# Two loads and two stores in turn with at most three transfers in flight, and two additions moved, in a group-norm and sign-weight convolution kernel

## What is computed

```python
bw = cw + stop_gradient(jnp.sign(W) - cw)          # the value is sign(W)
x = x + conv_general_dilated(_gn(x), bw, window_strides=(1, 1), padding=((1, 1), (1, 1)))
# _gn: mean and variance over a group of 2 channels x 56 x 56 pixels, eps 1e-5
```

## Time and profile before

| | us |
|---|---|
| timed runs, median of 3 | 204.43 (203.82 to 205.47) |
| the profiled execution, its own time | 206.21 |
| its span, first to last instruction | 204.4 |

### The profile page before, as it was taken

How to read it: one execution, slowest core, us unless ns; L and a number is a source line. 1 busy time by engine, 2 the same in 40 slices (tenths; PEclk the granted TensorE clock), 3 DMA queues, 4 the chain that set the end, 5 groups by cost and what they waited for, 6 DMA issues and landing times.

```text
span 204.4 us, 10027 instructions
## 1 busy us (share of the span) xinstructions
PE 191.5 (94%) x4482; PEld 168.2 (82%) x4482; DVE 165.5 (81%) x363; ACT 149.7 (73%) x142; POOL 166.7 (82%) x85
## 2 busy tenths in 40 slices
PE   1999999998999999999979999899989999999990
PEld 0587977887887887977868898799988999999990
DVE  2999999996999877999957799987769799727392
ACT  3186998899987299899429989943997999596000
POOL 1039887999999999989996988999798799999500
PEclk9999999999999999999999999999999999999997
DMA  6986878929798998988959988898887970905374
GB/s 215 373 336 207 262 244 255 305 92 323 295 314 258 352 327 282 266 246 342 305 231 251 308 246 225 340 289 259 273 247 231 232 274 3 387 18 233 120 270 174
DMA packets 18698, 52.17 MB, mean 255 GB/s; under 512 B 2080, under 2 KB 5024, under 8 KB 18656
## 3 DMA queue, kind: packets, MB, share of 16 engines
q1 hardware_dynamic: 18656, 51.54, 76.7%
HBM read 25.84 MB, written 25.69 MB: 252 GB/s over the span
## 4 chain that ended last, share of the span: by engine, by line
PE 69%; DVE 12%; ACT 10%; DMA 3%; issue 2%; POOL 1%; SPq 1%; DVEq 0%; ACTq 0%; POOLq 0%
PE psum L720 69%; DVE stats L487 4%; ACT halves L411 3%; ACT xnorm L405 3%; DMA w_raw<-in_L_conv_W_dram 3%; DVE xbuf L557 2%; DVE xbuf L543 1%; DVE xbuf L567 1%; POOL halves L320 1%; SPq L236 1%; ACT moved L424 1%; ACT line_halves L434 1%; DVE xbuf L531 1%; ACT lines_norm L438 1%; DVE own L495 1%
## 5 line engine op out<-in xcount | busy, mean ns | idle before, releaser
L720 PE MATMUL psum<-halves,w_taps 64*64 64x385 f16 (+8 forms) x4140 | 184.9, 325 | 3.2 <-issue 2.5
L720 PEld LDWEIGHTS psum<-halves,w_taps 64*64 64x64 f16 x4140 | 158.5, 107 | 21.2 <-issue 4.1
L320 POOL TENSOR_TENSOR halves<-xnorm,halves 128x784 f16<-128x784 f32 (+5 forms) x35 | 91.7, 2641 | 21.8 <-ACT xnorm L405 21.6
L487 DVE BATCH_NORM_STATS2 stats<-xbuf 128x6 f32<-128x448 f32 x112 | 60.7, 611 | 3.6 <-DMA xbuf<-in_x_dram 3.3
L411 ACT ACTIVATE halves<-xbuf,coef 128x784 f16<-128x784 f32 (+5 forms) x35 | 50.7, 1449 | 3.6 <-DVE coef L512 3.3
L405 ACT ACTIVATE xnorm<-xbuf,coef 128x784 f32<-128x784 f32 (+5 forms) x35 | 50.5, 1442 | 0.0
L424 ACT ACTIVATE moved<-psum 64x784 f32<-64x784 f32 (+1 forms) x30 | 25.5, 849 | 11.4 <-PE psum L720 10.8
L335 POOL TENSOR_TENSOR xbuf<-xbuf,moved 128x784 f32<-128x784 f32 (+1 forms) x15 | 29.4, 1957 | 2.0 <-ACT moved L424 2.0
L557 DVE SCALAR_TENSOR_TENSOR xbuf<-psum,xbuf 64x784 f32<-64x784 f32 (+1 forms) x32 | 28.2, 881 | 1.0
L543 DVE SCALAR_TENSOR_TENSOR xbuf<-psum,xbuf 128x784 f32<-128x784 f32 x21 | 20.3, 967 | 10.7 <-PE psum L720 10.7
L361 POOL TENSOR_TENSOR line_halves<-lines_norm,line_halves 128x1512 f16<-128x1512 f32 (+1 forms) x10 | 20.9, 2121 | 0.5 <-ACT lines_norm L438 0.2
(11 more groups left out here) (36 smaller groups left out, 72.5 us busy)
## 6 DMA issues: line engine op xcount, KB each, us to landing
xbuf<-in_x_dram SPq DMA_DIRECT2D x48, 448.0 KB, 4.9
out_dram<-xbuf SPq DMA_DIRECT2D x43, 392.0 KB, 4.7
xbuf<-in_x_dram SPq DMA_DIRECT2D x16, 224.0 KB, 5.1
out_dram<-xbuf SPq DMA_DIRECT2D x5, 504.0 KB, 5.9
out_dram<-xbuf SPq DMA_DIRECT2D x5, 448.0 KB, 3.2
out_dram<-xbuf SPq DMA_DIRECT2D x5, 364.0 KB, 5.3
out_dram<-xbuf SPq DMA_DIRECT2D x5, 252.0 KB, 5.0
out_dram<-xbuf SPq DMA_DIRECT2D x1, 224.0 KB, 2.9
```

The source lines that it names most:

```text
L320: nc.gpsimd.tensor_tensor(at(halves[:, k % HRING, 1, :], a, b), at(xnorm[:, k % NRING, :], a, b), at(halves[:, k % HRING, 0, :], a, b), AL ...
L487: nc.vector.bn_stats(stats[:, n, :], xbuf[:, s, n * STAT:(n + 1) * STAT]).then_inc(blocks_ready, 1)
L720: mm = pe.matmul(outs[:, :, left:right], weights, ins[:, :, left + dx:right + dx], start=first_step, stop=last_step)
```

## The change

- SP: the pieces of a pair are loaded two at a time. In loop k: pieces 0 and 1 of pair k+3 (when TensorE has finished the away blocks before pair k), then the two stores of the second half of pair k-1 (`store_unit(k - 1, 1)`), then pieces 2 and 3 (when two away blocks of pair k are done), then the two stores of the first half of pair k.
- SP: before each of these transfers it waits until the third last one has landed (`ended[-3]`), so that at most three are in flight. For that every store has a semaphore of its own (`stored[s][n]`), and the waits on them are by part. The last three stores of the last pair are not paced.
- SP: the loads of pair 2 are paced too; before, two of its pieces were issued with those of pair 1 and two later.
- `WINOGRAD` pairs are stored in other pieces: rows 43 to 56, 0 to 16, 16 to 34 and 34 to 43.
- GpSimd: where pair k is in `WINOGRAD` and pair k-2 is not (k = 3, 6, 9, 12), `add_away(k - 2, 1)` comes behind the chunks `lo(k, c)` instead of ahead of them.
- VectorE: in loop 1, three of the seven statistics of pair 3 come behind `add_home(1, 0)` and `add_away(1, 0)` instead of ahead.

The diff, its core:

```diff
@@ -181,7 +181,7 @@
         psum = ctx.enter_context(nc.psum_tensor("psum", [128, 8, 512], F32))
 
         loaded = [[sem(f"loaded{s}_{p}") for p in range(NPIECE)] for s in range(XRING)]
-        stored = [sem(f"stored{s}") for s in range(XRING)]
+        stored = [[sem(f"stored{s}_{n}") for n in range(5)] for s in range(XRING)]
         w_loaded = sem("w_loaded")
         w_signed = sem("w_signed")
         ident_step = sem("ident_step")
@@ -242,11 +242,18 @@
             sp.dma_start(w_raw[:], w.rearrange("o c h w -> o (c h w)")).then_inc(w_loaded, 16)
             for n in range(NPIECE):
                 start_load(sp, 1, n)
-            for n in range(2):
-                start_load(sp, 2, n)
-            def store(k, a, b):
-                sp.dma_start(at(both(out, k), a, b), at(xbuf[:, k % XRING, :], a, b)).then_inc(stored[k % XRING], 16)
+            ended = [(loaded[1][n], 16) for n in range(NPIECE)]
+            def load(k, n):
+                sp.wait_ge(*ended[-3])
+                start_load(sp, k, n)
+                ended.append((loaded[k % XRING][n], landed(k)))
+            def store(k, n, a, b):
+                sp.dma_start(at(both(out, k), a, b), at(xbuf[:, k % XRING, :], a, b)).then_inc(stored[k % XRING][n], 16)
 
             def wait_away(k, i):
                 u = away_before(k) + i
@@ -255,56 +262,59 @@
                 else:
                     sp.wait_ge(away_done, 2 * aways_before(u + 1))
 
-            def store_part(k, n):
+            def paced_store(k, n, a, b):
+                sp.wait_ge(*ended[-3])
+                store(k, n, a, b)
+                ended.append((stored[k % XRING][n], landed(k)))
+            def store_unit(k, i):
                 if k in WINOGRAD:
-                    if n == 0:
+                    if i == 0:
                         sp.wait_ge(home_done, home_before(k) + 1)
-                        store(k, WROW + WROWS, H)
-                    elif n == 1:
-                        wait_away(k, 0)
-                        store(k, 0, 16)
-                    elif n == 2:
-                        sp.wait_ge(home_done, home_before(k) + 3)
-                        store(k, WROW, WROW + WROWS)
-                    else:
-                        wait_away(k, 1)
-                        store(k, 16, WROW)
+                        paced_store(k, 0, WROW + WROWS, H)
+                        return
+                    wait_away(k, 0)
+                    paced_store(k, 1, 0, 16)
+                    sp.wait_ge(home_done, home_before(k) + 3)
+                    wait_away(k, 1)
+                    paced_store(k, 2, 16, WROW + 9)
+                    paced_store(k, 3, WROW + 9, WROW + WROWS)
                     return
-                sp.wait_ge(home_done, home_before(k) + n // 2 + 1)
-                wait_away(k, n // 2)
-                store(k, 14 * n, 14 * n + 14)
-            def wait_part(k, n):
-                if k in WINOGRAD and n == 3:
-                    sp.wait_ge(home_conv, home_blocks_before(k, 1) + 2)
-                elif k + n > 0:
-                    sp.wait_ge(away_conv, away_blocks_before(k) + n)
+                sp.wait_ge(home_done, home_before(k) + i + 1)
+                wait_away(k, i)
+                paced_store(k, 2 * i, 28 * i, 28 * i + 14)
+                paced_store(k, 2 * i + 1, 28 * i + 14, 28 * i + 28)
+            for n in range(NPIECE):
+                load(2, n)
             for k in range(NP):
-                for n in range(NPIECE):
-                    new = k + AHEAD
-                    if new < NP:
-                        if new >= XRING:
-                            sp.wait_ge(stored[new % XRING], 64 * (new // XRING))
-                        wait_part(k, n)
-                        start_load(sp, new, n)
-                    if n < 3 and k >= 1:
-                        store_part(k - 1, n + 1)
-                    elif n == 3:
-                        store_part(k, 0)
-                    elif n >= 1:
-                        start_load(sp, 2, n + 1)
-            store_part(LAST, 1)
+                new = k + AHEAD
+                if new < NP:
+                    if new >= XRING:
+                        for n in range(4):
+                            sp.wait_ge(stored[new % XRING][n], landed(new - XRING))
+                    if k:
+                        sp.wait_ge(away_conv, away_blocks_before(k))
+                    load(new, 0)
+                    load(new, 1)
+                if k >= 1:
+                    store_unit(k - 1, 1)
+                if new < NP:
+                    sp.wait_ge(away_conv, away_blocks_before(k) + 2)
+                    load(new, 2)
+                    load(new, 3)
+                store_unit(k, 0)
             for n, (first, rows) in enumerate(((28, 14), (42, 8), (50, 6))):
 
                 sp.wait_ge(home_done, home_before(LAST) + 2 + n)
                 sp.wait_ge(away_done, 2 * (aways_before(away_before(LAST) + 1) + 1 + n))
-                store(LAST, first, first + rows)
+                store(LAST, 2 + n, first, first + rows)
             for k in range(NP - XRING, NP):
-                sp.wait_ge(stored[k % XRING], 64 * (k // XRING + 1) + (16 if k == NP - 1 else 0))
+                for n in range(4):
+                    sp.wait_ge(stored[k % XRING][n], landed(k))
+            sp.wait_ge(stored[LAST % XRING][4], 16)
 
         @block.gpsimd
         def _(pool):
@@ -372,11 +382,14 @@
 
             for k in range(NP):
 
-                if k >= 2 and k - 2 not in WINOGRAD:
+                if k >= 2 and k - 2 not in WINOGRAD and k not in WINOGRAD:
                     add_away(k - 2, 1)
                 for c in range(len(chunks(k))):
                     if (k, c) != (0, 0):
                         lo(k, c)
+                if k >= 2 and k - 2 not in WINOGRAD and k in WINOGRAD:
+                    add_away(k - 2, 1)
                 if k == 0:
                     weights_of_products()
                 if k + 1 in WINOGRAD:
@@ -611,11 +624,16 @@
                 if k - 1 in WINOGRAD:
                     add_outer(k - 1)
                     add_away(k - 1, 1)
-                if 1 <= k < NP - 2:
+                if k == 1:
+                    pair_stats(3, range(4))
+                elif 1 <= k < NP - 2:
                     pair_stats(k + 2, range(NSTAT))
                 add_home(k, 0)
                 if k not in WINOGRAD:
                     add_away(k, 0)
+                if k == 1:
+                    pair_stats(3, range(4, NSTAT))
                 if k == 0:
                     pair_stats(2, range(NSTAT))
                 if k < NP - 2:
```

## The result

| | before | after |
|---|---|---|
| timed runs, median (range), us | 204.44 (203.82 to 208.49) | 212.68 (210.09 to 213.86) |
| the profiled execution, its own time, us | 206.21 | 213.05 |
| its span, us | 204.4 | 211.3 |

The changed kernel is slower: the ratio of the times is 1.035 [1.027, 1.043]. The direction was forecast, though narrowly; the size (206.7, with 203.4 to 210.0 as the range) was not.

What follows compares the result with a forecast made beforehand. TensorE was taken as the bound, busy 191.5 of 204.4 us. 206.21 - 3.5 + 2.5 + 2.1 = 207.3 us for an execution like the profiled one, 206.7 forecast for the runs; own range 205.0 to 208.6, overall 203.4 to 210.0.

Steps and rivals of the forecast that it cites:

- Part 1: SP's loads and stores: at most three in flight removes TensorE's three "issue" cuts, -3.5 us (bounds 0 and -3.67).
- Rival 2: Instruction fetches stay late: pacing cures nothing and the new waits come, 210.2 us; chance 0.13.
- Part 2, pair 3: Addition behind pair 3's lower halves delays loads and statistics of pair 5; TensorE pays +2.5 us at pair 4 (1.5 to 3.5).
- rival 1: The two loads behind the addition land before VectorE asks, so cuts and both waits go: 201.1 us; chance 0.13.
- landed at 3.8 or so: Pair 3: piece 3 of pair 5, issued at 52.4 us behind the first store, lands 3.8 us later, at 56.2.
- Part 2, pairs 6, 9 and 12: Moved addition delays loads, statistics and bank-freeing additions there: 0.7 us each, +2.1 us in all (bounds 0 and 1.4 each).
- Pair 9's own path: Addition ends at 117.7 us, statistics at 124.9, 1.75 late; add_inner(9) ends 1.3 later, costing pair 10 0.7 us.
- Rival 3: Only pair 3 pays; at pairs 6, 9 and 12 loads land 0.7 us sooner: 204.6 us; chance 0.14.
- Part 3: VectorE at pair 1: moving three statistics cures pair 2's 0.4 us wait, swallowed by pair 3's: 0 us, at best -0.4.
- the same 0.6 us taken off: Final sum: 207.3 us became 206.7, leaning two to one to 207.3 over 205.5 for the timed runs.

Runs made afterwards that it cites:

- e2: The kernel before with only the addition moved behind the lower halves at pairs 3, 6, 9 and 12: 210.06 us, ratio 1.028.
- e3: The changed kernel without the waits on the third last transfer; order of transfers and moved addition kept: 210.35 us, ratio 1.032.
- e5: The kernel before with only the cap of three transfers in flight added: 206.72 us, ratio 1.011.
- e12: The changed kernel with four transfers in flight for three; order and moved addition kept: 211.77 us, ratio 1.040.
- e8: The changed kernel with the addition ahead of the lower halves again at pair 3 alone: 206.9 us, ratio 1.016.
- e4: The changed kernel with SP's loads of pieces 2 and 3 put ahead of store_unit(k - 1, 1), cap kept: 202.12 us, ratio 0.989.
- e10: e4 with all seven statistics of pair 3 ahead of the additions of pair 1 again: 201.49 us, ratio 0.989.
- e11: The same kernel as e4, run again: 202.35 us, ratio 0.994.
- e6: e4 without its cap on transfers in flight: 203.66 us, ratio 1.000.

## Why the prediction was right in its path and wrong in its size

I compare by pairs, from TensorE's first matmul of a pair to that of the next, read in its timeline. A `WINOGRAD` pair takes 10.53 us where nothing stops it.

**Part 1: the size came out (-3.5 forecast, -3.8 measured) between the two profiled executions; its cause is not shown.** The ordinary pairs that had lost time to cuts (7, 10 and 11) are back at 11.82 to 11.84 us; together that is -3.8. But they are back in e2 and e3 as well, where no cap stands. And the profiled execution before was a late one, 1.78 us over its median: e1, which keeps the cap and undoes the moved addition, is at 0.997 [0.991, 1.002] of before in the timed runs, so at most 0.9% or 1.8 us was won there on balance. By the turn-taking that the Trainium skill ("DMA: Bandwidth & Descriptors", section on queues, rings and completion order) describes, this part would have been worth 0. The runs don't decide it: a packet of instructions ends ahead of each cut, but the number of transfers in flight doesn't tell which packet brings one. Rival 2 did not come true, since the cuts are gone in the changed kernel; that its 210.2 us lies nearer to 212.68 than the forecast is chance. The cap also has a price of its own, which the forecast put at nothing: e5, and pair 3 below.

**Part 2, pair 3: the path was right, the term (+2.5) mis-sized; it measured +5.5.** GpSimd's and SP's timelines of the changed kernel:

```profile
43.32 4.61 POOL L330 TENSOR_TENSOR halves<-xnorm,halves 128x1456 f16<-128x1456 f32 x2
47.89 1.85 POOL L345 TENSOR_TENSOR xbuf<-xbuf,moved 128x784 f32<-128x784 f32 x1
```

```profile
49.80 0.82 SPq L256 DMA_DIRECT2D out_dram<-xbuf  x2
50.72 1.81 SPq L236 DMA_DIRECT2D xbuf<-in_x_dram  x2
```

The addition ends at 49.74 (49.6 forecast) and refutes rival 1. The stores go out at once, piece 2 of pair 5 at 50.7 (50.45), piece 3 at 52.19 (52.4). Up to here the steps hold to within 0.3 us. VectorE's timeline, pair 3 and then pair 9:

```profile
55.09 1.15 DVE L500 BATCH_NORM_STATS2 stats<-xbuf 128x6 f32<-128x448 f32 x2 [2.92 <-DMA xbuf<-in_x_dram]
57.84 0.63 DVE L500 BATCH_NORM_STATS2 stats<-xbuf 128x6 f32<-128x448 f32 x1 [1.60 <-DMA xbuf<-in_x_dram]
58.38 0.96 DVE L544 SCALAR_TENSOR_TENSOR xbuf<-psum,xbuf 128x392 f32<-128x392 f32 x2
...
60.14 2.44 DVE L587 SCALAR_TENSOR_TENSOR xbuf<-psum,xbuf 128x504 f32<-128x504 f32 x4
...
130.09 1.92 DVE L500 BATCH_NORM_STATS2 stats<-xbuf 128x6 f32<-128x448 f32 x3 [1.89 <-DMA xbuf<-in_x_dram]
131.92 0.96 DVE L544 SCALAR_TENSOR_TENSOR xbuf<-psum,xbuf 128x392 f32<-128x392 f32 x2
133.68 2.44 DVE L587 SCALAR_TENSOR_TENSOR xbuf<-psum,xbuf 128x504 f32<-128x504 f32 x4
```

*Step that failed: "landed at 3.8 or so".* Piece 2 landed at 55.1, as forecast; piece 3 not at 56.2 but at 57.8, 5.6 us after its issue (the chain's 5.63). `add_inner(3)` then ends at 60.14 + 2.44 = 62.58 instead of 61.1: 1.5 us. What the DMA engines did, and what TensorE did next, in stretches of the changed kernel (columns as in e3's):

```profile
57.20:58.70 1.50, 0.00 (x0) 0.00 (x0) 0.86 (x2) 0.00 (x0) 1.50 (x1) 0.63 0.07 26
59.40:64.00 4.60, 4.60 (x44) 2.04 (x48) 3.95 (x12) 2.56 (x4) 4.19 (x2) 0.50 0.92 352
```

From 57.2 to 58.7 us the DMA engines are busy for 0.07, about one of sixteen. Piece 3 lands within that stretch, at 57.8, and SP issues the next load only then, at 57.88. The cap holds everything else back while few engines finish. In e3, without the cap, the share in the gap is 1.03. Why those engines were behind is open: no row shows it. Nor is it shown that the cap made this load slow: from issue to landing the same piece took 5.1 us in e3 and 5.8 in e12, where the DMA engines were busy. There it was issued at 50.9 us, 1.3 earlier, and that is what the cap took here; the 3.8 us for the landing were too few in all three.

*A price that stood in no term: the clock.* TensorE was idle from 55.48 to 59.40, and in that gap the granted clock fell (mean 0.63 from 57.2 to 58.7), then stayed at 0.50 up to 64 us, the lower of its two levels (1.2 instead of 2.4 GHz). TensorE's timeline, pair 3 (its matmuls, then the first weight load of pair 4) and then pair 9:

```profile
59.40 0.63 PE L738 MATMUL psum<-line_halves,w_taps 64*64 64x504 f16 x2 [3.92 <-DVE xbuf L544]
59.82 0.63 PE L738 MATMUL psum<-line_halves,w_taps 64*64 64x495 f16 x2
...
64.43 1.61 PEld L738 LDWEIGHTS psum<-halves,w_taps 64*64 64x64 f16 x40 [0.22 <-issue]
...
132.94 0.40 PE L738 MATMUL psum<-line_halves,w_taps 64*64 64x504 f16 x2 [1.25 <-DVE xbuf L544]
...
136.18 0.52 PE L738 MATMUL psum<-halves,w_taps 64*64 64x392 f16 x6 [0.49 <-DVE xbuf L587]
```

The steps follow each other by 0.42 us where the kernel before has 0.21 (its last product is at 58.36, its pair 4 starts at 58.57). The twelve that are left of pair 3 take 5.03 us instead of 2.55, and pair 4 begins at 64.43. At full clock they would have ended at 61.95, and pair 4 could have begun when `add_inner(3)` ended, at 62.58: the clock costs 64.43 - 62.58 = 1.85 us in this execution. Not every run paid it: in the fastest, 210.09 us, the granted clock over the span is 0.998, in the profiled one 0.984. So pair 4 is 3.3 us behind the forecast's 61.1: 1.5 by the landing, 1.85 by the clock. Against before it starts 64.43 - 58.57 = 5.9 us later, 0.4 of them because the first matmul of the whole kernel came 0.4 us later: +5.5. The Trainium skill ("TensorE: Matmul & The Clock Gate", Part 1) lists the same two levels, the lower one after idling; the trace agrees with its 0.50 behind this gap.

**Part 2, pairs 6, 9 and 12: the term (+2.1) mis-sized; +1.2, +2.2 and +1.6, in all +5.0.** Pair 9's own path in the forecast: addition ended 0.2 us before the pair begins, statistics 7.2 us later, all of it paid at pair 10. GpSimd's and ScalarE's timelines at pair 9:

```profile
117.48 4.61 POOL L330 TENSOR_TENSOR halves<-xnorm,halves 128x1456 f16<-128x1456 f32 x2 [2.27 <-ACT xnorm L418]
122.03 1.88 POOL L345 TENSOR_TENSOR xbuf<-xbuf,moved 128x784 f32<-128x784 f32 x1
```

```profile
112.30 0.29 ACT L413 ACTIVATE std<-own,eps 128x1 f32<-128x1 f32 x1 [5.12 <-DVE own L508]
```

The addition ends at 123.91, 0.4 us *after* the pair's start at 123.47, so 0.6 us later than forecast. The lower halves waited 2.27 us for ScalarE (1.25 before). ScalarE's `std` of pair 9 had waited 5.12 us for an aggregate, and the last statistic ahead of that aggregate 1.37 us for a load; before, the same `std` waited 3.69 us. The rows of VectorE in the changed kernel and of ScalarE before:

```profile
107.95 0.63 DVE L500 BATCH_NORM_STATS2 stats<-xbuf 128x6 f32<-128x448 f32 x1 [1.37 <-DMA xbuf<-in_x_dram]
...
103.18 0.29 ACT L400 ACTIVATE std<-own,eps 128x1 f32<-128x1 f32 x1 [3.69 <-DVE own L495]
```

A late load thus delays the next addition, and that the next loads: the forecast took the times of ScalarE in the earlier trace rows as fixed. The statistics then end 8.1 us behind the addition (130.09 + 1.92 = 132.01), 0.9 more than forecast, the loads being later. TensorE pays at `add_home(9, 0)`, 1.25 us, where the forecast had no wait, and at `add_inner(9)`, 0.49 (its weight loads, which show the beginning of a gap better, have 1.73 and 0.96). Together 0.6 + 0.9 = 1.5 us over the forecast's 0.7, which is the 2.2 of pair 9. Rival 3 (these pairs cost nothing) is refuted, by e8 too.

**Part 3 fits its forecast of 0.** In e4's order the split wins nothing (e10 is not slower than e11). In the changed kernel the wait at pair 2 is gone, and pair 3's own waits follow it; no run takes the split alone out of that kernel.

**Sum.** 206.21 - 3.8 + 5.5 + 5.0 + 0.4 (the later first matmul, whose cause was not looked for) = 213.3 us; the execution took 213.05. The forecast had -3.5 + 2.5 + 2.1. The failure is in two terms, both too small because the delay was costed once, with the landing times of an undisturbed queue, ScalarE's old times and a full clock. Its upper bound for pair 3, 3.5 us, held neither a load of 5.6 us behind two stores nor the clock. Nor does the forecast's own range follow from its bounds: added up at their ends, with the same 0.6 us taken off, they give 203.6 to 209.8 us and not 205.0 to 208.6. The measured time lies outside both.

## What to carry to other kernels

Before a producer is moved later, look which in-order queue waits for its result and what stands behind that wait: here loads stood behind a store, and putting them ahead of it (e4) turned a loss of 3.5% into a gain of about 1%. A wait that TensorE meets costs more than its length where the clock falls in it, so a forecast that makes a gap of several microseconds needs a second bound with the clock at half. A cap on transfers in flight goes with fewer cuts but can make loads late: where loads were early it gained up to about 1% (e4 and e11 against e6, the second within the noise), and in front of late loads it cost (e5). A gain that is read from one profiled execution should be checked against the timed runs before it goes into a sum (part 1).

## What the runs showed of the hardware

- With at most three transfers in flight, the DMA share fell to 0.07 for 1.5 us while one load was finishing, and that load took 5.6 us from issue to landing; without a cap (e3), or with four in flight (e12), the share in the same gap was 1.03 and 1.00, and the same load took 5.1 and 5.8 us.
- The granted clock fell in a gap of 3.9 us and was 0.50 over the matmuls from 59.40 to 64.00 us. In the profiled gaps of 2.4 us (e3) and 2.8 us (e12) at the same place it stayed at 1.00. It differs between executions of one kernel: over the span the six runs of the changed kernel have 0.984 to 0.998.
- TensorE stopped for 0.5 to 1.6 us nine times in fourteen traces where the profile names nothing that it waited for, and each time went on 1.2 to 1.5 us after the end of a packet on the instruction queue. Most of these cuts are in traces without a cap, but e3, with up to nine transfers in flight at such a packet, has none.
